# Graph kernel on one core: gathers that land in the tile of use, an ordering moved into the gate stage, and a node table that carries its degree factor

## The chip, the core and the metric
The kernel runs on one core of one Trainium2 chip. The metric is the device time of one execution in microseconds. The engines are TensorE (PE, with its weight loads as PEld), VectorE (DVE), ScalarE (ACT), GpSimd (POOL) and SyncE (SP); L-numbers are lines of the kernel's file.

## What is computed
100,000 nodes with 48 features, 25,000 edges (src, dst), the edges ordered by dst. Four layers, each added to its input and normalised over the 48 features:

```python
x = LN(x + L0(x)); x = LN(x + L1(x)); x = LN(x + L2(x)); x = LN(x + L3(x))
# L0: (1+eps)*x + segment_sum(relu(x[src] + ea48), dst)
# L1: msg = x[src] * rsqrt(max(out_deg,1))[src]
#     agg = segment_sum(msg, dst) * rsqrt(max(in_deg,1))
#     relu(where(in_deg>0, agg, x) @ W.T + b)
# L2: dis = rsqrt(deg) where deg>0 else 0 (deg counts src)
#     relu(segment_sum(dis[src]*dis[dst]*x[dst], src) @ W.T + b)
# L3: gate = silu(ea40 @ W1.T + b1) @ W2.T + b2
#     gate += sum(emb[type[src]] * (emb[type[dst]] @ adaptW.T))
#     msg = gate * h[dst] * (cutoff(weight) * node_vec[dst])
#     h + segment_sum(msg, src) / max(segment_sum(node_vec[dst], src), 1e-8), layer norm, gamma, beta
```

## The kernel before, in words
**Layout.** The edges lie as 128 partitions x 196 columns (`EP = 25088`), handled in 14 chunks of H = 14 columns or 7 blocks of R = 28. The nodes are 28 dense blocks of 128 x 28 x 48, worked in pairs (h = 0, 1). Node tables in DRAM: `xa_table` (XA: x, type, place and degree of each node, 52 wide), `x_table` and `y_table` (X1, Y1: the state after layer 0 and the same times the degree factor, 48 wide; X2 after layer 1), `edge_records`, `records_by_src`, `h_by_src` for layers 2 and 3.

**Gathers and scatters.** A gather of 128 rows is one indirect DMA, issued by GpSimd; a whole one is 196 of them. All gathers go through `ring`, two halves of 14 columns: `gather_turn` (L420) waits for `ring_free`, issues 14 DMAs into half c % 2, and a consumer empties it. For the gathers of x by src, of XA by dst and of X2 by src the consumer is ScalarE: `source_rows` (L606), the loop with `take` (L555) and `rows_of_src` copy the half to `XS`, `zs`, `nv`, `zd`, `place` and `dg`, and give the half back. For the gather of y it is `take_terms` (L535), which writes the transposed terms that VectorE's scan reads. A scatter (`scatter`, L456) sends 14 rows of `stage`, which ScalarE fills in `to_stage` (L594) from M or XS, and only rows that are the last of their segment are written.

**The stages in order of time.** (a) VectorE counts sources by 196 comparisons of one column with 128 numbers (`L1179`), a product of one-hots on TensorE gives the degree of each node; meanwhile GpSimd gathers x by src. (b) ScalarE writes the degrees into the node rows that SP streams through `din` (`degrees`, L616), SP stores XA; meanwhile VectorE orders the edges by source: `sort` (L1042), a bitonic network of 120 comparisons (two instructions each, L1065 and L1066) and 14 turns by TensorE on the array `va`/`vb`, which lies inside the tile `do`. (c) VectorE sums the messages of layer 0 (L1218 and a scan, 14 times). (d) Pass 1: norm of x for all nodes, times `deg` for Y1 (L1303), two stores per block; beside it GpSimd gathers XA by dst. (e) Seven update blocks (`xs` of the nodes at dst; the product by the root of the degree) and the scatter of y; pass 2, which multiplies each block of X1 by the weights on TensorE and stores X2, runs beside the scatter. (f) The gather of y and the gate of layer 3: 49 groups of four columns. In a group VectorE makes the two one-hots of the next group (L1359), TensorE transposes them (L933), multiplies by `logit` (L945), by the first weights (L950) and by the second (L955), and VectorE combines (L1372 to L1379). In groups 0 and 4 of each block VectorE also scans the terms of one chunk. (g) Updates, the scatter into X2; (h) gather of the records, ordering of them; gather of X2 by src, of H2 into `ring`, the last sums and the scatter into the output.

**What sets the order.** Every engine runs its own program, written out in this order; they meet in semaphores only. SP issues the loads and stores of `din` and `do`/`dy` in a fixed sequence, also the store of the ordered keys (`SRT`) before pass 1.

```python
            def gather_turn(table, w, of, c, **skip):
...
            def take(h, uses):

                act.wait_ge(fill[h].sem, fill[h].up(H))
                for to, of in uses:
                    nc.scalar.activation(to, of, ACT.Copy).then_inc(own.sem, own.add())
                act.wait_ge(own.sem, own.now())
                act.sem_inc(S["ring_free"], 1)
                act.sem_inc(S["kept"], 1)
```

## Time and profile before

| | |
|---|---|
| runs | 3299.1, 3349.46 and 3291.38 us (median 3299.1) |
| profiled execution | 3287.26 us, span 3285.5 us |
| busy, share of the span | POOL 59%, DVE 62%, PE 23%, ACT 19% |
| the chain that ended last | DVE 28%, POOL 24%, issue 19%, PE 12%, another core or an unknown queue 9%, ACT 5%, DMA 3% |
| DMA | mean 82 GB/s; 56,448 packets of indirect DMAs |

POOL's busy time is the time of its 1768 instructions, the greater part of them issues of indirect DMAs. "Issue" in the chain is time in which the engine waited for nothing that the profile shows. "Another core or an unknown queue" stands for a release whose origin the profile can't name; on a group of rows it reads "remote". The clock of TensorE is granted at 0.5 of full speed in most slices.

### The profile page before, as it was taken

Reading aid. Unit: us, or ns where it says so; the run is one execution under the profiler, and the core shown is the slowest. Engines: PE = TensorE matmul, PEld = TensorE weight load, DVE = VectorE, ACT = ScalarE, POOL = GpSimd, SP = SyncE. Lnnn points to the kernel's source line nnn. Section 1 sums busy time; section 2 is a strip of 40 time slices with the busy share of each in tenths; the row PEclk is TensorE's granted clock in tenths of the full one; section 3 lists DMA queues with packets and bytes.
Section 4 is the critical chain, followed back from the end, with each engine's and each line's share of the span. In section 5 each row is a group of like instructions: output and inputs, shape, how many; then the busy total and the mean of one; then the engine's idle time right before and its main releaser. Section 6 shows DMA issues by size and latency. Waiting matters only on the chain.

```text
span 3285.5 us, 13920 instructions
## 1 busy us (share of the span) xinstructions
PE 766.0 (23%) x3478; PEld 542.8 (17%) x3478; DVE 2024.3 (62%) x2590; ACT 622.5 (19%) x1021; POOL 1932.9 (59%) x1768
## 2 busy tenths in 40 slices
PE   1182000000166663877742300000340000000000
PEld 0020000000155552544431300000340000000000
DVE  2186279977865564545452470788658969948551
ACT  0000101221122231322211100222111223221110
POOL 5704623774055657564326773777757777673776
PEclk7586555555565565555555555555555555555555
DMA  3106703763033331110000099344222212210000
GB/s 110 21 1 243 277 27 137 273 223 144 0 108 109 131 120 56 26 25 22 20 10 14 15 82 85 117 135 135 76 69 67 83 57 80 66 52 7 16 15 15
DMA packets 154357, 268.53 MB, mean 82 GB/s; under 512 B 87656, under 2 KB 112314, under 8 KB 154146
## 3 DMA queue, kind: packets, MB, share of 16 engines
q1 hardware_dynamic: 92786, 198.90, 20.8%
q0 software_dynamic: 56448, 44.04, 6.7%
q10 hardware_dynamic: 5040, 24.69, 2.0%
q8 instruction: 28, 0.46, 0.1%
q14 instruction: 55, 0.45, 0.0%
HBM read 135.62 MB, written 137.21 MB: 83 GB/s over the span
## 4 chain that ended last, share of the span: by engine, by line
DVE 28%; POOL 24%; issue 19%; PE 12%; another core or an unknown queue 9%; ACT 5%; DMA 3%; SPq 0%; ACTq 0%; DVEq 0%; POOLq 0%
POOL ring L424 10%; POOL out L462 6%; POOL x_table L462 5%; POOL y_table L462 3%; DVE mu L1259 2%; DVE var L1268 2%; DVE du L1262 2%; PE psA L897 2%; DVE sumb L1205 2%; PE psO L859 2%; PE psA L950 1%; PE psT L844 1%; DVE du L1471 1%; DVE do L1467 1%
## 5 line engine op out<-in xcount | busy, mean ns | idle before, releaser
L462 POOL DMA_INDIRECT y_table<-sumb,put x196 | 214.7, 1095 | 258.6 <-ACT sumb L594 201.0
L462 POOL DMA_INDIRECT x_table<-sumb,put x196 | 216.4, 1104 | 180.6 <-ACT sumb L594 117.8
L424 POOL DMA_INDIRECT ring<-xa_table,dstI x196 | 216.9, 1106 | 171.9 <-ACTq L561 101.7
L424 POOL DMA_INDIRECT ring<-in_xaux,srcI x196 | 186.3, 950 | 207.9 <-ACTq L561 116.8
L424 POOL DMA_INDIRECT ring<-edge_records,dstI x196 | 227.9, 1163 | 102.0 <-issue 61.3
L424 POOL DMA_INDIRECT ring<-y_table,srcI x196 | 201.4, 1028 | 137.6 <-ACTq L544 78.9
L424 POOL DMA_INDIRECT ring<-h_by_src,zd x196 | 230.1, 1174 | 87.4 <-issue 61.0
L424 POOL DMA_INDIRECT ring<-x_table,srcI x196 | 224.4, 1145 | 90.9 <-issue 58.1
L462 POOL DMA_INDIRECT out<-sumb,put x196 | 214.6, 1095 | 106.8 <-issue 60.8
L1268 DVE TENSOR_REDUCE var<-sq 128x28 f32<-128x1344 f32 x119 | 181.1, 1551 | 143.0 <-ACT sq L567 142.8
L830 PE MATMUL psG<-ident,tail 128*49 128x128 f32 x10 | 4.3, 433 | 1086.9 <-DVEq L1011 1086.9
L567 ACT ACTIVATE sq<-du 128x1344 f32<-128x1344 f32 x126 | 164.5, 1320 | 450.5 <-DVE du L1262 420.2
L830 PEld LDWEIGHTS psG<-ident,tail 128*49 128x49 f32 x10 | 1.5, 154 | 1089.3 <-DVEq L1011 1072.9
L844 PE MATMUL psT<-ident,din 128*96 128x128 f32 x392 | 96.1, 395 | 294.8 <-DMA din<-x_table 294.6
L586 ACT ACTIVATE hT<-psT 96x512 f32<-96x512 f32 (+1 forms) x168 | 88.8, 537 | 377.2 <-PE psT L844 190.3
L859 PE MATMUL psO<-w1b,hT 97*128 97x96 f32 x504 | 107.6, 386 | 147.1 <-ACT hT L586 141.0
L1179 DVE TENSOR_SCALAR GX<-GX 128x128 bf16<-128x128 int16 x196 | 49.3, 252 | 125.1 <-remote 113.3
L859 PEld LDWEIGHTS psO<-w1b,hT 97*128 97x128 f32 x504 | 99.8, 295 | 155.9 <-ACT hT L586 147.4
L844 PEld LDWEIGHTS psT<-ident,din 128*96 128x96 f32 x392 | 73.0, 200 | 298.0 <-DMA din<-x_table 295.8
L1259 DVE TENSOR_REDUCE mu<-du 128x28 f32<-128x1344 f32 x70 | 106.1, 1549 | 3.0
L1262 DVE SCALAR_TENSOR_TENSOR du<-mu,du 128x1344 f32<-128x1344 f32 x70 | 106.6, 1555 | 1.4
L1205 DVE TENSOR_TENSOR_SCAN sumb<-mask,sub 128x720 f32<-128x720 bf16 x56 | 92.8, 1657 | 17.3 <-ACT sub L528 9.1
(280 smaller groups left out, 3013.9 us busy)
## 6 DMA issues: line engine op xcount, KB each, us to landing
din<-in_xaux SPq DMA_DIRECT2D x56, 728.0 KB
x_table<-do SPq DMA_DIRECT2D x56, 672.0 KB
din<-x_table SPq DMA_DIRECT2D x56, 672.0 KB
xa_table<-din SPq DMA_DIRECT2D x28, 728.0 KB
y_table<-GX SPq DMA_DIRECT2D x28, 672.0 KB
out<-do SPq DMA_DIRECT2D x28, 672.0 KB
records_by_src<-ring ACTq DMA_DIRECT2D x14, 693.0 KB
GX<-records_by_src ACTq DMA_DIRECT2D x14, 693.0 KB
```

The lines of the kernel that those rows point to most:

```text
L424: pool.indirect_dma_start(ring[:, h, t, 0:w], None, table, bass.IndirectOffsetOnAxis(ap=of[:, c * H + t:c * H + t + 1], axis=0), **skip).t ...
L462: pool.indirect_dma_start(table, bass.IndirectOffsetOnAxis(ap=put[:, c * H + t:c * H + t + 1], axis=0), stage[:, h, t, :], None, bounds_ch ...
L567: nc.scalar.activation(sq[:, h, :, :], u, ACT.Square).then_inc(S["squared"], 1)
L586: nc.scalar.activation(hT[0:96, g % 2, 0:w], psT[g % 2][0:96, 0:w], ACT.Copy).then_inc(S["hT_ready"], 1)
L844: last = T.transpose(psT[g % 2][0:96, j * P:(j + 1) * P], rows_of[:, (4 * g + j) * 96:(4 * g + j + 1) * 96], ident[:, :])
L859: last = T.matmul(psO[k % 6][:, j * 96:(j + 1) * 96], hT[0:97, g % 2, j * P:(j + 1) * P], weights[:, :], start=True, stop=True)
L897: last = T.matmul((psA, psB)[c][:, 0:CN // 2], ohp[:, g, :], ohc[:, g, c * (CN // 2):(c + 1) * (CN // 2)], start=start, stop=stop, skip_gr ...
L1179: V.tensor_scalar(ohp[:, g, :], iota[:, 0:P], parf[:, bass.ds(i * R + t, 1)], None, ALU.is_equal)
L1205: return V.tensor_tensor_scan(sums_row[:, part], mask_row, terms_row[:, part], 0.0, ALU.mult, ALU.add)
L1259: V.tensor_reduce(mu[:, h, :], x, X, ALU.add).then_inc(own.sem, own.add())
L1262: V.scalar_tensor_tensor(u, along(mu[:, h, :]), -1.0 / D, x, ALU.mult, ALU.add).then_inc(S["centered"], 1)
L1268: V.tensor_reduce(var[:, h, :], sq[:, h, :, :], X, ALU.add).then_inc(S["var_ready"], 1)
```

## The change
It does three things. The three node gathers named above land at once in one tile, `XD` (128 x 196 x 52), of which `XS` is the first 48 columns: `gather_in_place` has one semaphore for each chunk (`rows0` to `rows13`) and no ring half. The gather of XA waits at each chunk for `xs_free` (the sum of layer 0 over this chunk is done), that of X2 for `by_src` (the ordering of the records). The copies of ScalarE for them are gone. The ordering by source leaves stage (b) and becomes a generator, of which VectorE does up to six steps ahead of each of the gate's 49 groups; the turns by TensorE come at 14 fixed groups; the keys are stored behind the gate. `deg` is turned into the degree factor before XA is built, X1 and `x1_with_degree` (Y1) are 49 wide and hold x and the factor; the two products (L1303, and `M` by the root) are gone, VectorE multiplies the messages by the factor as it forms the terms in the gate (`messages`), and pass 2 multiplies by `w1c`, which has a zero row for the factor. ScalarE stages the rows of the y scatter between the updates (`STAGED`) and between the pairs of pass 2 (`STAGED_LATER`).

```diff
+            rows, xs_free = views(*ROWS), views("xs_free")[0]
+            def gather_in_place(table, w, of, free=None):
+                for c in range(CE // H):
+                    if free:
+                        pool.wait_ge(free.sem, free.up())
+                    for t in range(c * H, c * H + H):
+                        pool.indirect_dma_start(
+                            XD[:, t, 0:w], None, table, bass.IndirectOffsetOnAxis(ap=of[:, t:t + 1], axis=0)
+                                ).then_inc(rows[c].sem, rows[c].add())
...
-            gather(A["xaux"], XW, srcI)
+            gather_in_place(A["xaux"], XW, srcI)
             pool.wait_ge(S["xa_done"], 1)
-            gather(XA, XW, dstI)
+            gather_in_place(XA, XW, dstI, xs_free)
             pool.wait_ge(idx_ready.sem, idx_ready.up())
             pool.wait_ge(short_done.sem, short_done.up())
-            scatter(Y1)
-            gather(Y1, D, srcI)
+            scatter(Y1, stage1)
+            gather(Y1, YW, srcI)
...
+            def to_stage1(i):
+                act.wait_ge(rows_new.sem, rows_new.up())
+                for h in range(2):
+                    cols = bass.ds((2 * i + h) * H, H)
+                    act.wait_ge(stage_free.sem, stage_free.up())
+                    nc.scalar.activation(stage1[:, h, :, 0:D], XS[:, cols, :], ACT.Copy).then_inc(own.sem, own.add())
+                    nc.scalar.activation(stage1[:, h, :, D], XD[:, cols, D + 3], ACT.Copy).then_inc(own.sem, own.add())
+                    act.wait_ge(own.sem, own.now())
+                    act.sem_inc(S["rows_ready"], 1)
+            STAGED = {0: 0, 3: 1, 6: 2}
             for i in range(NBLK):
                 norm([(0, su[:, :, :])])
+                if i in STAGED:
+                    to_stage1(STAGED[i])
+            STAGED_LATER = {1: 3, 2: 4, 4: 5, 5: 6}
...
+            one(V.tensor_scalar(none, deg, 1.0, None, ALU.min))
+            one(V.tensor_scalar(deg, deg, 1.0, None, ALU.max))
+            ask_act()
+            one(V.reciprocal(deg, deg))
+            one(V.tensor_tensor(deg, deg, none, ALU.mult))
             dve.sem_inc(S["deg_done"], 1)
...
-            sort(own, ask_pe)
-            dve.sem_inc(S["srt_ready"], 1)
...
                     for h in range(2):
-                        V.tensor_tensor(dy[:, h, :, :], DO[h],
-                                        along(deg[:, bass.ds((PER * i + 2 * q + h) * R, R)]), ALU.mult
-                                        ).then_inc(S["out_ready"], 1)
+                        V.tensor_copy(do1[:, h, :, D], deg[:, bass.ds((PER * i + 2 * q + h) * R, R)]
+                                      ).then_inc(own.sem, own.add())
...
+            ordering, turns = sort(own, ask, answered, pos2), sort_groups()
+            def sort_on(g):
+                if g + 1 in turns:
+                    return
+                for _ in range(QUOTA):
+                    if next(ordering, "end") in ("turn", "end"):
+                        break
+            def factors(g):
+                sort_on(g)
+                if g + 1 < GROUPS:
+                    one_hots(g + 1)
+                if g % (R // 4) in (0, 4):
+                    messages(g % (R // 4) // 4)
...
+            def messages(h):
+                dve.wait_ge(fill[h].sem, fill[h].up(H))
+                V.tensor_tensor(terms[:, h, :, 1:H + 1].rearrange("p d c -> p c d"), ring[:, h, :, 0:D],
+                                along(ring[:, h, :, D]), ALU.mult).then_inc(ring_read.sem, ring_read.add())
+                dve.wait_ge(ring_read.sem, ring_read.now())
+                dve.sem_inc(S["ring_free"], 1)
+                summed(h, 2)
```

GpSimd at its first gather and the start of the second, before (`srcI` and `dstI` are the indices, `xa_done` SP's word that XA is stored):

```order
19 L424 DMA ring<-in_xaux,srcI 128x52 [waits ring_free,edges]
20 L424 DMA ring<-in_xaux,srcI 128x52 x13
21 L424 DMA ring<-in_xaux,srcI 128x52 [waits ring_free]
22 L424 DMA ring<-in_xaux,srcI 128x52 x13
23 L424 DMA ring<-in_xaux,srcI 128x52 [waits ring_free]
...
47 L424 DMA ring<-xa_table,dstI 128x52 [waits xa_done,ring_free,fill1,fill0]
48 L424 DMA ring<-xa_table,dstI 128x52 x13
49 L424 DMA ring<-xa_table,dstI 128x52 [waits ring_free]
```

GpSimd at the same place after the change:

```order
19 L465 DMA XD<-in_xaux,srcI 128x52 [waits edges]
20 L465 DMA XD<-in_xaux,srcI 128x52 x195
21 L465 DMA XD<-xa_table,dstI 128x52 [waits xs_free,xa_done]
22 L465 DMA XD<-xa_table,dstI 128x52 x13
23 L465 DMA XD<-xa_table,dstI 128x52 [waits xs_free]
```

The first gather has no wait between its 196 DMAs any more, the second waits for the sums of layer 0 in place of the ring.

VectorE behind the degrees, before (`GX` holds the degrees and ranks there, `do` the array being ordered):

```order
776 L1193 TENSOR_SCALAR GX<-deg 128x784 [waits dve]
777 L1194 TENSOR_SCALAR GX<-GX,carry 128x784 [waits dve]
778 L1195 TENSOR_TENSOR GX<-GX 128x784 [waits dve]
779 L1048 CAST do<-do 98x256 [waits dve]
780 L1049 MEMSET do 32x256 [waits dve]
781 L1050 TENSOR_SCALAR do<-do 98x256 [waits dve]
```

VectorE at the same place after the change:

```order
779 L1215 TENSOR_TENSOR GX<-GX 128x784 [waits dve]
780 L1216 TENSOR_SCALAR GX<-GX 128x784 [waits dve]
781 L1217 TENSOR_SCALAR GX<-GX 128x784 [waits dve]
782 L1219 RECIPROCAL GX<-GX 128x784 [waits dve,act_done]
783 L1220 TENSOR_TENSOR GX<-GX 128x784 [waits dve]
784 L1240 TENSOR_TENSOR sub<-MG,XD 128x14x48 [waits dve,rows0,ea48]
785 L1243 CAST mask<-cont 128x48x14
```

The factor stands ahead of the release of ScalarE's copy, and the sums of layer 0 follow at once, without the ordering.

VectorE in the gate, one group before (`L1359` makes the one-hots of the next group):

```order
1612 L1359 TENSOR_TENSOR du<-iotaz,du 128x480 [waits dve]
1613 L1359 TENSOR_TENSOR sq<-iotaz,du 128x480
1614 L1372 TENSOR_TENSOR sq<-psB,sq 128x480 [waits dve,mlp_o]
1615 L1374 TENSOR_REDUCE lg<-sq 128x4 [waits dve]
1616 L1376 TENSOR_TENSOR do<-psG,lg 128x192 [waits mlp_g,dve]
1617 L1379 TENSOR_TENSOR GX<-do,t1 128x4x48 [waits dve]
```

VectorE in the gate, one group with steps of the ordering after the change (one-hots are `L1380`):

```order
1370 L1082 TENSOR_SCALAR do<-do 128x16x8 [waits dve]
1371 L1082 TENSOR_SCALAR do<-do 128x8x16 [waits dve]
1372 L1070 TENSOR_TENSOR do<-do 128x16x8 [waits dve]
1373 L1071 TENSOR_TENSOR do<-do 128x16x8
1374 L1070 TENSOR_TENSOR do<-do 128x32x4 [waits dve]
1375 L1071 TENSOR_TENSOR do<-do 128x32x4
1376 L1380 TENSOR_TENSOR du<-iotaz,du 128x480 [waits dve]
1377 L1380 TENSOR_TENSOR sq<-iotaz,du 128x480
1378 L1410 TENSOR_TENSOR sq<-psC,sq 128x480 [waits dve,mlp_o]
1379 L1412 TENSOR_REDUCE lg<-sq 128x4 [waits dve]
1380 L1414 TENSOR_TENSOR do<-psT1,lg 128x192 [waits mlp_g,dve]
1381 L1417 TENSOR_TENSOR GX<-do,t1 128x4x48 [waits dve]
```

The steps stand ahead of the one-hots, for which TensorE waits; a group can hold six of them.

## Rows read from the trace of the kernel before

**Rows 1.** Groups by line: busy us, mean ns of one, idle us before them with releasers.

```profile
L424 POOL DMA_INDIRECT ring<-xa_table,dstI x196 | 216.9, 1106 | 171.9 <-ACTq L561 101.7 <-issue 64.6 <-SPq L336 5.6
L462 POOL DMA_INDIRECT y_table<-sumb,put x196 | 214.7, 1095 | 258.6 <-ACT sumb L594 201.0 <-issue 57.6
L424 POOL DMA_INDIRECT ring<-in_xaux,srcI x196 | 186.3, 950 | 207.9 <-ACTq L561 116.8 <-issue 67.4 <-DMA do<-in_src 23.7
...
L1179 DVE TENSOR_SCALAR GX<-GX 128x128 bf16<-128x128 int16 x196 | 49.3, 252 | 125.1 <-remote 113.3 <-issue 8.5 <-PE psB L897 3.0
```

**Rows 2.** Stretches: length, then busy us of PE, PEld, DVE, ACT, POOL, clock, DMA.

```profile
526.00:785.00 259.00, 0.00 (x0) 0.00 (x0) 219.78 (x168) 63.26 (x121) 190.19 (x168) 0.50 0.67 237
900.00:1257.00 357.00, 220.83 (x1140) 203.67 (x1139) 224.54 (x246) 106.08 (x176) 214.71 (x196) 0.61 0.33 113
1271.00:1640.00 369.00, 263.14 (x1195) 166.07 (x1195) 169.63 (x287) 105.45 (x149) 191.58 (x188) 0.50 0.11 24
```

**Rows 3.** Stretches of L1179 alone (counts): length, DVE busy (x), clock, DMA.

```profile
41.00:179.00 138.00, 7.05 (x26) 0.51 0.11 19
179.00:261.00 82.00, 39.84 (x160) 0.95 0.00 1
```

**Rows 4.** Timeline of VectorE, two comparisons: start us, us, instruction, idle before.

```profile
330.61 0.29 DVE L1065 TENSOR_TENSOR do<-do 128x128 f32<-128x128 f32 x1 [1.61 <-remote]
...
404.60 0.29 DVE L1065 TENSOR_TENSOR do<-do 128x128 f32<-128x128 f32 x1
```

**Rows 5.** Stretches of L1259 alone (one for each norm of a block).

```profile
797.00:886.80 89.80, 9.32 (x6) 0.50 0.00 0
1016.90:1052.10 35.20, 3.01 (x2) 0.50 0.27 91
1052.10:1069.00 16.90, 3.01 (x2) 0.85 0.32 115
```

**Rows 6.** Timeline from the degrees to pass 1, ScalarE, GpSimd and VectorE.

```profile
268.77 0.26 ACT L616 ACTIVATE din<-GX 128x28 f32<-128x28 f32 x1 [137.03 <-DVEq L1196]
...
400.21 0.94 POOL L424 DMA_INDIRECT ring<-xa_table,dstI  x1 [5.59 <-SPq L336]
...
516.86 5.05 DVE L1233 RECIPROCAL deg<-deg 128x784 f32<-128x784 f32 x1 [0.98 <-ACT deg L600]
```

**Rows 7.** Stretch of L616 alone (degrees into node rows, two a pair of blocks).

```profile
277.00:303.00 26.00, 1.56 (x6) 0.50 0.95 350
```

**Rows 8.** Stretches of L1303 alone (two a pair), and last one of L1218.

```profile
538.90:651.40 112.50, 21.18 (x14) 0.50 0.78 278
651.40:793.00 141.60, 21.19 (x14) 0.50 0.61 219
...
446.00:516.00 70.00, 18.18 (x14) 0.50 0.06 23
```

**Rows 9.** Timeline of TensorE and VectorE in one group of the gate.

```profile
1609.56 1.94 PE L955 MATMUL psT<-wm,do 49*128 49x48 f32 x8 [0.26 <-ACT do L679]
1611.43 1.38 PE L945 MATMUL psO<-logit,do 120*128 120x120 bf16 x12
1612.74 1.94 PE L950 MATMUL psA<-din,wm 40*48 40x512 f32 x2
1613.09 0.65 DVE L1359 TENSOR_TENSOR sq<-iotaz,du 128x480 bf16<-128x480 bf16 x1
1614.61 0.68 PE L933 MATMUL psO<-identb,du 128*120 128x128 bf16 x4
```

**Rows 10.** Groups by line: the terms of y by ScalarE, the sum in layer 0.

```profile
L540 ACT ACTIVATE sub<-ring 128x672 f32<-128x672 f32 x14 | 20.0, 1431 | 7.0 <-DMA ring<-y_table,srcI 6.5
L1218 DVE TENSOR_TENSOR sub<-MG,XS 128x672 f32<-128x672 f32 x14 | 18.2, 1298 | 0.7 <-DVE do L1066 0.2
```

**Rows 11.** Timeline of VectorE at the update of layer 2 and the last sums.

```profile
2470.44 1.56 DVE L1524 TENSOR_TENSOR du<-XS,MG 128x1344 f32<-128x1344 f32 x1 [10.75 <-ACTq L756]
...
2662.92 0.86 DVE L1535 TENSOR_TENSOR du<-ring,GX 128x672 f32<-128x672 f32 x1 [11.37 <-DMA ring<-h_by_src,zd]
```

More of the change, by code:

```diff
@@ L20 @@
 XW = 52
+YW = D + 1
 RW = 99
@@ L223, in bass_gnn @@
         psO = [ps("psO0"), ps("psO1"), psA, psB, psC, psG]
+        ROWS = tuple(f"rows{c}" for c in range(CE // H))
         S = {n: sem(n) for n in (
@@ L447, in gather_records, with scatter @@
                     gather_turn(REC, RW, of, c)
-            def gather_x2(of):
-                for c in range(2):
-                    ring_used(c)
-                    gather_turn(X2, D, of, c)
-                gather(X2, D, of, first=2)
-            def scatter(table):
+            def scatter(table, rows_of=stage):
                 for c in range(CE // H):
@@ L1385, in _ @@
+            for g in range(GROUPS):
+                factors(g)
+            for _ in ordering:
+                pass
+            dve.sem_inc(S["srt_ready"], 1)
             dve.wait_ge(returned.sem, returned.up(2 * NBLK))
```

439 lines of the change are left out of this document (213 added, 226 removed).

## The prediction
> **What bounds the kernel now.** I read the page's groups first. GpSimd issues nine rounds of 196 indirect DMAs, seldom more than 0.3 us apart, and stands still only where another engine holds it up: 116.8 us in the first gather (a free ring half, which ScalarE gives), 101.7 us in the second (the same), 201.0 us in the y scatter (staged rows) [rows 1]. The undisturbed pace is (186.3+67.4)/196 = 1.29 us, and between instructions 1.25 us. Nine rounds at 1.25 to 1.45 us are 2205 to 2558 of 3285 us, so no single engine is the bound: the chain hands over from stage to stage. Next the stages [rows 2]: pass 1 (526 to 785) has VectorE at 220 of 259 us; pass 2 (900 to 1257) and the gate (1271 to 1640) have no full engine. There the rows in time matter. A count takes 0.51 us when GpSimd is silent (160 in 82 us) and 5.3 us while it gathers (26 in 138 us) [rows 3], and of the 125.1 us that the counts' line stood idle 113.3 are put down to "remote" [rows 1]. A comparison of the ordering (two instructions) takes 0.53 us when undisturbed and 2.1 us next to table copy and gather, 1.61 of it again "remote" [rows 4]. A pair of pass 2 took 35.2 us under a scatter and 16.9 us with GpSimd idle [rows 5]. I read this as one effect: **while GpSimd issues without a pause, streams of short instructions on the other engines are starved**, some 17 us after it starts and up to 15 us after it stops (counting was slow from 41 to 179 us, GpSimd issued from 24 to 164 us). Long instructions aren't touched: pass 1 kept its pitch under 164 us of gathering. The change removes the pauses of GpSimd, so this effect decides.
>
> **Step 1, the count and the first gather.** The gather no longer waits for ring halves; it runs from 24.2 us for 196 x 1.25 = 245 us, to 269 instead of 164 us with a second part later. That removes the wait of 116.8 us, but not from the path: who ends last is the count, since the table copy needs degrees. In 105 us more of gathering 105/5 = 21 counts are made, which take 10.5 us otherwise: +94 us. The trace has no count under a longer gather; the bounds are 0 (only the first 140 us starve) and +105 (nothing is done); the row is the same gather, so +94. The degree factor (two TENSOR_SCALARs, a root, the reciprocal of 784 columns, a product) now stands ahead of the copy: the reciprocal alone is 5.1 us [rows 6], with the rest +8. Degrees are ready at 268.7+94+8 = 371 us.
>
> The Trainium skill ("Runtime: NRT & Kernel Launch", section "Instruction fetch mechanics") says that instructions are streamed in blocks by a DMA queue of the engine's own and that this fetch is mostly hidden. By that rule alone short streams would not slow, and the count would end as before; that is rival A below.
>
> **Step 2, the table copy.** 268.8 to 400.2 us before, 131 us or 9.4 a pair of blocks [rows 6]. Its first three pairs, mostly without the gather, took 26 us, 8.7 each, with DMA at 0.95 [rows 7]. Now nothing is gathered beside it: 14 x 8.5 = 118 us (bounds 118 and 131). The copy ends at 489 us, +89. The ordering by source is gone from VectorE here, and the sums of layer 0 (14 of them, 70 us [rows 8]) fit under the copy: nothing.
>
> **Step 3, pass 1 and the second gather.** Pass 1 begins at 494 us (before 525.8). A pair of blocks took 16.1 us (seven in 112.5), then 20.2 us (seven in 141.6) where ScalarE stood in take() for rows [rows 8]; both go, and so does the product for y: 2 x 1.51 = 3.0 us less (21.18 us for 14), 0.4 us for two short copies: 13.5 us x 14 = 189 us, end 683 (at 14.5 us: 697). DMA has room: 0.67 share at 259 us [rows 2] is 173 us of work. The gather runs beside it at 1.45 us: 285 us, 489 to 774 us. Before it ended at 785: **a wait of 101.7 us is gone, yet only 11 us are won**, for the start is later. What is won is behind it: the seven update blocks (15.0 us each, six in 89.8 [rows 5], 13.5 without the product for y) lie under the gather, so the scatter starts at 776, not 900.7 us: -125 us for GpSimd.
>
> **Step 4, staging.** ScalarE stages block 1 in the middle of the updates and needs the ring halves that the scatter frees. The first is free when chunk 0 has landed (776+22), the second after chunk 1 (817). Until then ScalarE squares nothing, VectorE waits in update 4 (it would be there at 740). Updates 4 to 6 end at 850, the second half of block 2 at 857; pass 2 starts then, against 893 us: -36 us. The lead of 125 us shrinks, since the scatter at 1.40 us a DMA rules the stage.
>
> **Step 5, pass 2.** GpSimd now scatters without the 83 us in which it waited, and gathers two chunks of y behind: busy from 857 to some 1120 us, short waits for staging included. At 31 us a pair (between 22.5 and 35.2) that is 8.4 pairs, the other 5.6 at 17 us: end at 1215, with ScalarE's waits for halves 1225 us, as against 1262 us: **-37**, no more. Bounds: 1185 (25 us) to 1250 us. In the product the 97th row of a transpose costs nothing visible.
>
> **Step 6, the gate.** Undisturbed, a group is 6.0 us, all TensorE: 1.94+1.38+1.94+0.68 [rows 9]. 49 groups are 294 us; the stage took 369, so 75 us are starvation, 28 of them in one burst of 42 gathers. Now each of 34 groups gets up to six steps of the ordering between GX of the last group and the one-hots of the next. TensorE waits for these one-hots; their slack is 0.9 us (ready at 1613.7, used at 1614.61). The 165 steps are 120 comparisons x 0.53, 14 copies and some 31 short ones: 79 us; 34 x 0.9 = 30 us are hidden, so +50 us. Transposes for the turns: 14 x 0.9, half hidden, +5. The messages move from ScalarE (1.43 us) to VectorE (1.30 us, the row of the like sum of layer 0) [rows 10]: a group can hide 2.4 us of it, a group with steps 1.3: +20 us. Of starvation the long burst goes (-28), but VectorE issues nearly twice as many instructions while GpSimd gathers (18 of 29 us a chunk): I take 70 us, bounds 0 and 150. Sum: 294+50+5+20+70 = 439 us, **+70**. The stage ends at 1232+439 = 1671, before at 1640: +31.
>
> **Step 7, the rest.** One root, one reciprocal of 196 columns and three short operations are gone ahead of the third scatter: -4 us. Storing the ordered keys moves behind the gate on SP's queue, beside updates that wait for nothing of SP: 0 (bound +4). The last gather of x2 goes in place: VectorE's wait of 10.75 us goes and the h2 gather starts some 33 us earlier, which saves the two waits of 11.4 us [rows 11]; its own pace then holds the second chunk: -28 us at the dense pairs, and so at the end. Against it, the product stage there (84 TensorE rows in 15 us) loses the pauses of GpSimd: +8 (0 to 30).
>
> **The sum**: -39 up to the gate (-37 and 2 us of its head), +70, -4, -20 = **+7 us** on 3287 us of the profiled execution, which lies 12 us under the median of 3299. I predict 3294 us, no difference that can be told. (Some 2%, 66 us, is what a measurement of this kernel separates from no change.)
>
> **Rivals.** A: the count isn't slowed by a longer gather. For it: it recovered at 179 us by itself, and 440 instructions then ran at full speed, the last 20 us of them beside a gather. Against: each stretch of slow counts lies within GpSimd's issuing plus 15 us. Then all to the third scatter comes 94 us earlier: 3200 us. It decides once the extra delay stays under 20 us. Chance 0.2.
> B, slower: the ordering is starved in the gate as it was beside the table copy. 120 comparisons at 2.1 instead of 0.53 us are +188 us; the gate has GpSimd silent for a third of the time, so +125, less the 30 us I have already put in for it: 3390 us. For it: the ordering's instructions are as short as the counts, and they stand in the stage with the most of them. Against: pauses of 5 us were enough to refill. It decides when a comparison costs over 1.0 us on average. Chance 0.17.
> C: pass 2 and gate go on at undisturbed speed, for starvation belongs to the table traffic: pass 2 ends at 857+14 x 18 = 1110, gate 369 us: 3294-115-70 = 3110 us. The slow pair at 35.2 us with DMA at a third speaks against it: 0.04.
>
> **Chances.** 0.59 for mine (3230 to 3360 by the bounds of steps 5 and 6). The range takes in A and most of B: 3200 to 3385. Faster by over 2%: A, C and a tail of mine, 0.26; within 2%: 0.53; slower: 0.21.
>
> **What would show it.** First gather ends near 269 us with no wait; degrees at 370 us (A: 277); copy's end at 489; first y scatter at 776; update 4 of pass 1 waiting some 70 us for ScalarE; first matmul of pass 2 at 857; gate from 1232 to 1671, groups with steps 8.2 us apart; h2 gather 33 us nearer to the record gather's end. I am wrong if the counts keep 0.5 us after 180 us, or if the gate is far from 439 us.

## The result and the profile after
The changed kernel took 3524.2 us (median of 4 runs, 3508.4 to 3545.4), the kernel before 3324.3 us (median of 4, 3291.4 to 3377.1): ratio 1.070, 95% interval 1.060 to 1.080. It is slower by 7%; I had forecast no difference, 3294 us. The profiled execution took 3508.4 us (span 3506.6), 221 us more than the 3287.3 us of the one before. In two of the experiments below, e5 and f4, one of the four executions was slow by over 4%; the medians given contain it (3150.7 and 3064.1 us without it), the ratios don't.

The groups by line of the profile after, GpSimd's first and then two of VectorE's (busy us, mean ns, idle us before them with releasers); they answer to [rows 1]:

```profile
L452 POOL DMA_INDIRECT ring<-h_by_src,zs x196 | 233.4, 1191 | 317.9 <-ACTq L783 186.4 <-DMA h_by_src<-MG 73.6 <-issue 57.9
...
L465 POOL DMA_INDIRECT XD<-xa_table,dstI x196 | 221.5, 1130 | 292.6 <-SPq L361 233.2 <-issue 59.4
...
L495 POOL DMA_INDIRECT x_with_degree<-sumb,put x196 | 200.3, 1022 | 106.1 <-issue 60.5 <-ACTq L647 45.5
L465 POOL DMA_INDIRECT XD<-x_table,srcI x196 | 191.4, 977 | 59.8 <-issue 59.8
L465 POOL DMA_INDIRECT XD<-in_xaux,srcI x196 | 188.1, 960 | 85.2 <-issue 60.0 <-DMA t<-in_ew 25.1
...
L1199 DVE TENSOR_SCALAR GX<-GX 128x128 bf16<-128x128 int16 x196 | 51.5, 263 | 228.3 <-remote 177.6 <-issue 48.0 <-PE psB L892 2.5
L1557 DVE TENSOR_SCALAR MG<-psO 128x384 f32<-128x384 f32 x14 | 7.8, 558 | 178.7 <-remote 111.5 <-issue 39.6 <-PE psO L854 27.6
```

The three in-place gathers wait for no ring half any more, as the change says: apart from the first start (25.1 us) and the wait for the table copy, their idle time is "issue". What was 116.8 and 101.7 us of waiting for ring halves is gone. In its place stand 233.2 us for the table copy, and in the last gather (H2) 73.6 us for the stored products and 186.4 us for ring halves, where before 24.1 and 2.3 us were waited. The counts (L1199) stood idle 228.3 us, before 125.1. The last row is the product stage of layer 2, in which TensorE multiplies seven blocks while X2 is gathered: its 14 rows waited 178.7 us. In the kernel before the same group reads:

```profile
L1515 DVE TENSOR_SCALAR MG<-psO 128x384 f32<-128x384 f32 x14 | 7.8, 557 | 43.9 <-PE psO L859 40.2 <-remote 3.7
```

The stretches of the two lines in the profile after: counts in the first two rows ([rows 3] of before), the product stage in the third:

```profile
41.00:290.00 249.00, 14.05 (x50) 0.51 0.12 21
300.00:369.00 69.00, 35.46 (x138) 0.97 0.00 1
...
2394.00:2692.00 298.00, 13.21 (x26) 0.50 0.12 29
```

50 counts in 249 us, 5.0 us each, and 138 in 69 us, 0.50 each, once GpSimd (silent from 273.7 us) lets go. The product stage took 298 us for what it did in 94 us before (2343 to 2437 us). The points that the prediction named, in time, with their idle times:

```profile
385.35 0.26 ACT L626 ACTIVATE din<-GX 128x28 f32<-128x28 f32 x1 [6.19 <-DVEq L1221]
...
506.88 0.95 POOL L465 DMA_INDIRECT XD<-xa_table,dstI  x1 [233.16 <-SPq L361]
...
788.14 1.01 POOL L495 DMA_INDIRECT x_with_degree<-sumb,put  x1 [0.31 <-issue]
...
827.34 1.55 DVE L1287 TENSOR_REDUCE var<-sq 128x28 f32<-128x1344 f32 x1 [60.33 <-ACT sq L582]
...
866.94 2.02 PE L854 MATMUL psO<-w1c,hT 98*128 98x96 f32 x8 [146.62 <-ACT hT L601]
...
1317.96 0.65 PE L922 MATMUL psO<-identb,du 128*120 128x128 bf16 x4 [24.53 <-DVEq L1383]
...
2698.35 1.89 POOL L452 DMA_INDIRECT ring<-h_by_src,zs  x1 [73.58 <-DMA h_by_src<-MG]
...
2898.17 1.47 POOL L452 DMA_INDIRECT ring<-h_by_src,zs  x1 [154.30 <-ACTq L783]
```

Read down: degrees at 385 us (forecast 371), copy done by 507 (489), scatter of y at 788 (776), the wait of 60 us in an update for ScalarE (forecast some 70), pass 2 at 867 (857): up to here the forecast holds within 18 us. The gate began at 1317 us (forecast 1232). It ended at 1722 us, and in the kernel before at 1651 us: 71 us behind. When the gather of X2 begins the kernel is 51 us behind the one before (2373.9 against 2323.0 us); my sum had +27 there. The rest, 170 us, arises behind it, where my sum had -20. Its terms are in the rows: 73.6 + 186.4 - 24.1 - 2.3 = 234 us more waiting of the H2 gather, less 64 us by which the gather of X2 is shorter (251 against 315 us), 170 us. The norms and dense pairs (2698 to 2898 us), which had lain beside the gather of X2, now lay behind the late product stage, and the ring halves could only be refilled after them.

How the product stage crawls, in the timeline of ScalarE, VectorE and TensorE (start, us, instruction, idle before). TensorE transposes `sub` in lots of four (`psT`), ScalarE copies them to `hT`, TensorE multiplies `hT` into `psO`, `psA` or `psB`, and VectorE takes the product out:

```profile
2447.32 0.36 DVE L1557 TENSOR_SCALAR MG<-psB 128x192 f32<-128x192 f32 x1 [10.64 <-issue]
...
2452.67 1.94 PE L840 MATMUL psT<-ident,sub 128*96 128x128 f32 x8 [31.78 <-issue]
2458.51 0.59 ACT L601 ACTIVATE hT<-psT 96x512 f32<-96x512 f32 x1 [38.85 <-issue]
2459.16 2.02 PE L854 MATMUL psO<-w2b,hT 97*128 97x96 f32 x8 [4.54 <-issue]
2460.98 1.06 PE L840 MATMUL psT<-ident,sub 128*96 128x128 f32 x4
2469.72 0.59 ACT L601 ACTIVATE hT<-psT 96x512 f32<-96x512 f32 x1 [10.61 <-issue]
...
2492.11 0.56 DVE L1557 TENSOR_SCALAR MG<-psO 128x384 f32<-128x384 f32 x1 [39.55 <-issue]
2503.32 0.59 ACT L601 ACTIVATE hT<-psT 96x512 f32<-96x512 f32 x1 [33.01 <-issue]
...
2525.72 0.56 DVE L1557 TENSOR_SCALAR MG<-psO 128x384 f32<-128x384 f32 x1 [33.04 <-remote]
2531.32 0.38 ACT L601 ACTIVATE hT<-psT 96x256 f32<-96x256 f32 x1 [27.41 <-remote]
...
2553.72 0.56 DVE L1557 TENSOR_SCALAR MG<-psA 128x384 f32<-128x384 f32 x1 [27.44 <-remote]
2564.91 0.36 DVE L1557 TENSOR_SCALAR MG<-psB 128x192 f32<-128x192 f32 x1 [10.64 <-remote]
```

TensorE starts 0.06 us after ScalarE's copy has ended (2459.10), so that direction isn't slow. The other one is. The eight transposes of 2452.67 us are two lots of four; ScalarE copies the first 4.8 us after its end by the profile (2453.8) and the second 15.1 us after (2454.6 to 2469.7), though it stood idle for 10.6 us of that. VectorE takes the first product 30.9 us after it ended by the profile (2461.2 to 2492.1).

The starts follow a simple count. ScalarE and VectorE go on at intervals of 11.2, 22.4, 11.2, 22.4, 5.6, 22.4 and 11.2 us (2458.51 to 2564.91), and between the results that they wait for lie 4, 8, 4, 8, 2, 8 and 4 instructions of TensorE (transposes or products): **2.8 us for each instruction of TensorE**, for transposes and products alike. A count is two of its instructions, and takes 5.6 us (VectorE starts them at 104.32, 109.91, 115.52 us). A block of this stage is 42, and the last result of one block and of the next are taken at 2447.32 and 2564.91 us: 117.6 us, 42 times 2.8. The traces of a and f1 below have the same intervals. The semaphore events in the trace say on which side the delay lies: while counts crawl, TensorE's signal is given 4.1 us after its product has ended by the profile (median of 42 counts; 0.01 us where nothing crawls), and VectorE starts 0.02 us after the signal. So the waiting engine is ready and the signal is late. The profile models the ends of TensorE's instructions, so whether the result or only its signal is late can't be told from it.

### The profile page after: what moved, and what is told of

It is laid out like the page before. It is cut to its first block, busy times and chain, and to the rows that moved or that the text cites. A ratio compares the mean times of both kernels' runs of the same rounds, so it can differ in the third digit from the quotient of the medians.

```text
span 3506.6 us, 13765 instructions
## 1 busy us (share of the span) xinstructions
PE 780.9 (22%) x3478; PEld 560.1 (16%) x3478; DVE 1996.2 (57%) x2610; ACT 569.2 (16%) x906; POOL 1899.0 (54%) x1768
## 3 DMA queue, kind: packets, MB, share of 16 engines
q1 hardware_dynamic: 93060, 200.27, 19.3%
## 4 chain that ended last, share of the span: by engine, by line
DVE 25%; POOL 23%; issue 20%; another core or an unknown queue 13%; PE 10%; DMA 5%; ACT 4%; SPq 0%; ACTq 0%; DVEq 0%; POOLq 0%
POOL XD L465 6%; POOL out L495 6%; POOL x_table L495 5%; POOL ring L452 3%; POOL x_with_degree L495 3%; DVE mu L1278 2%; DVE du L1281 2%; DVE var L1287 2%; DMA din<-in_xaux 2%; PE psT L840 2%; PE psO L854 2%; DMA xa_table<-din 1%; PE psA L892 1%; DVE do L1512 1%
## 5 line engine op out<-in xcount | busy, mean ns | idle before, releaser
L452 POOL DMA_INDIRECT ring<-x_with_degree,srcI x196 | 205.5, 1048 | 376.4 <-DVEq L1426 318.5
L452 POOL DMA_INDIRECT ring<-h_by_src,zs x196 | 233.4, 1191 | 317.9 <-ACTq L783 186.4
L465 POOL DMA_INDIRECT XD<-xa_table,dstI x196 | 221.5, 1130 | 292.6 <-SPq L361 233.2
L495 POOL DMA_INDIRECT x_with_degree<-sumb,put x196 | 200.3, 1022 | 106.1 <-issue 60.5
L465 POOL DMA_INDIRECT XD<-in_xaux,srcI x196 | 188.1, 960 | 85.2 <-issue 60.0
L465 POOL DMA_INDIRECT XD<-x_table,srcI x196 | 191.4, 977 | 59.8 <-issue 59.8
L601 ACT ACTIVATE hT<-psT 97x512 f32<-97x512 f32 (+3 forms) x168 | 88.9, 540 | 598.7 <-remote 220.0
L1199 DVE TENSOR_SCALAR GX<-GX 128x128 bf16<-128x128 int16 x196 | 51.5, 263 | 228.3 <-remote 177.6
L840 PE MATMUL psT<-ident,din 128*97 128x128 f32 x392 | 98.6, 401 | 273.6 <-DMA din<-x_table 273.4
L854 PE MATMUL psO<-w1c,hT 98*128 98x96 f32 x392 | 85.0, 392 | 250.6 <-ACT hT L601 201.1
L840 PEld LDWEIGHTS psT<-ident,din 128*97 128x97 f32 x392 | 79.6, 267 | 275.6 <-DMA din<-x_table 275.6
L1557 DVE TENSOR_SCALAR MG<-psO 128x384 f32<-128x384 f32 x14 | 7.8, 558 | 178.7 <-remote 111.5
```

The costliest lines, as they stand in the source:

```text
L452: pool.indirect_dma_start(ring[:, h, t, 0:w], None, table, bass.IndirectOffsetOnAxis(ap=of[:, c * H + t:c * H + t + 1], axis=0), **skip).t ...
L465: pool.indirect_dma_start(XD[:, t, 0:w], None, table, bass.IndirectOffsetOnAxis(ap=of[:, t:t + 1], axis=0)).then_inc(rows[c].sem, rows[c]. ...
L495: pool.indirect_dma_start(table, bass.IndirectOffsetOnAxis(ap=put[:, c * H + t:c * H + t + 1], axis=0), rows_of[:, h, t, :], None, bounds_ ...
L601: nc.scalar.activation(hT[0:tall, g % 2, 0:w], psT[g % 2][0:tall, 0:w], ACT.Copy).then_inc(S["hT_ready"], 1)
L840: last = T.transpose(psT[g % 2][0:tall, j * P:(j + 1) * P], rows_of[:, at:at + tall], ident[:, :])
L854: last = T.matmul(psO[k % 6][:, j * 96:(j + 1) * 96], hT[0:tall + 1, g % 2, j * P:(j + 1) * P], weights[:, :], start=True, stop=True)
```

## The experiments
**Two kinds of chip.** The executions fell on several chips, and they differ. On some the kernel before takes 3177 to 3324 us (medians) and shows the 5 us counts; on others it takes 2905 to 2919 us and counts take 0.5 us under the gather. I call the first kind starving, and set the ratio only between runs taken together on one chip. The five groups of experiments ran on five chips, one after the other, and none of these came twice: that the difference belongs to the chip, and not to the hour, is my reading and not shown. The first four experiments fell on a chip that doesn't starve, so what they expected of starvation could not be seen there; they gave something else, the price of each part without it.

**Hold in the gather of X2 (e1), hold in the first gather (e2), both (e4).** The edit, on the changed kernel:

```diff
                 for c in range(CE // H):
+                    if c in holds:
+                        pool.wait_ge(S[holds[c][0]], holds[c][1])
...
+            gather_in_place(A["xaux"], XW, srcI, holds={8: ("deg_done", 1)})          # e2, e4
+            gather_in_place(X2, D, srcI, holds={2: ("h2_ready", 2), 3: ("h2_ready", 4), 4: ("h2_ready", 6),
+                                                5: ("h2_ready", 7)})                  # e1, e4
```

> The changed kernel, but in the in-place gather of X2 chunks 2, 3, 4 and 5 wait until blocks 2, 4, 6 and 7 of the product stage are done, as the ring made them wait before. Theory S (unbroken issuing by GpSimd starves short instructions): the product stage takes 106 to 125 us in place of 315 us, the gather of X2 315 us in place of 251 us, so the gather of H2 starts at about 2700 us as now but is no longer held for 154 us; its end comes 160 to 180 us earlier, the kernel takes 3330 to 3350 us. Theory R (the loss sits in the prefilled ring halves and the order of ScalarE's work, not in the stream): the product stage shortens by less than 60 us or the hold of 154 us stays, and the time stays above 3450 us.

> The changed kernel, but the first gather stops after eight chunks (112 DMAs) until the degrees are ready. Theory S: counts recover at about 180 us, the degrees and their factor are ready at 277 us in place of 385, the table copy takes 131 us in place of 118, the scatter of y starts at 690 to 700 us in place of 788; the kernel takes 3405 to 3430 us. The rival (the lead is lost again in pass 2 and the gate, where other things end last): scatter of y at 700, but the kernel stays over 3480 us.

> The changed kernel with both holds, in the first gather and in the gather of X2. If both losses are starvation and add up, 3230 to 3265 us, some 1% under the kernel before (3287 us profiled). If the rest of the change is a loss of its own, over 3300 us.

Measured, not starving: e1 2946.4 us, ratio 1.012 (1.010 to 1.014); e2 2923.2 us, 1.0045 (1.003 to 1.006); e4 2947.3 us, 1.013 (1.011 to 1.015). The hold of e2 is void there: the degrees are ready at 155 us, before the gather comes to chunk 8 (its 196 DMAs run from 25.3 to 293.9 us with no gap), so e2 stands for the changed kernel. Where nothing starves, then, the change costs 12 us, and holding the gather of X2 costs 23 us more and gives nothing. What the three runs were to decide, how much each hold gives back, stayed undecided there.

**The ordering behind the gate (e3).**

```diff
-                if g + 1 in turns:
+                if g < GROUPS:
                     return
```

(and TensorE's 14 turns behind its last group).

> The changed kernel with all 165 steps of the ordering and its 14 turns in one piece behind the last group of the gate, where GpSimd is silent. My working of the prediction: the gate's groups shorten by 55 us (from 405 to 350 us), and the ordering costs 105 to 115 us by itself: 50 to 60 us slower in all, 3560 to 3585 us. Rival (the steps are starved inside the gate): the gate's groups shorten by more than 100 us, and the time is the same as the changed kernel or less.

Measured: 2951.5 us, ratio 1.014 (1.011 to 1.017). The gate of e2 and of e3 in stretches (length, then PE, PEld, DVE, ACT, POOL busy, clock, DMA), first e2, with its pass 2:

```profile
650.00:969.00 319.00, 222.41 (x1166) 214.78 (x1167) 214.51 (x239) 103.78 (x179) 170.83 (x166) 0.61 0.37 124
993.00:1342.00 349.00, 279.37 (x1268) 178.68 (x1268) 270.27 (x599) 89.48 (x138) 178.46 (x168) 0.50 0.13 24
```

and e3:

```profile
990.00:1278.00 288.00, 273.12 (x1240) 172.53 (x1240) 195.17 (x314) 84.90 (x137) 183.59 (x168) 0.50 0.16 29
```

The steps cost the groups 61 us (I had 50 + 5), and 14 us of 75 us of VectorE's work (270.27 - 195.17) are hidden in them. Behind the gate the ordering makes the kernel 28 us slower than inside (expected 50 to 60). That bears out my working of the steps' own cost. It says nothing on the rival, starved steps, for nothing starves on this chip; f3, f4, e6 and e9 below decide that.

**The kernels on a starving chip (b, a, e4b, e5).** The edit of e5, waits for landing in the in-place gathers:

```diff
                                 ).then_inc(rows[c].sem, rows[c].add())
+                    pool.wait_ge(rows[c].sem, rows[c].now())
```

> The kernel before, unchanged, for a trace beside the experiments. Two conditions are possible. Where short instructions are starved while GpSimd issues (as in the two traces that I compared): 3290 to 3350 us, counts at 5 us under the gather. Where they are not (as in the first four experiments, where the kernel before took 2912 us): 2905 to 2915 us, counts at 0.5 us throughout.

> The changed kernel, unchanged. Starved: 3500 to 3545 us, ratio 1.06 to 1.08. Not starved: the product stage takes some 91 us under the gather of X2, the gate's groups 350 us, and the time is that of the run with a hold in the first gather, 2915 to 2930 us, ratio 1.00 to 1.01, since without starvation this hold ends before the gather comes to it.

> Both holds again. Starved: 3230 to 3265 us if both losses are starvation and add up, over 3300 us if the rest of the change is a loss of its own. Not starved: 2940 to 2950 us, 25 us over the changed kernel, which is the price of the hold in the gather of X2.

> The changed kernel, but GpSimd waits after each chunk of 14 in-place DMAs until they have landed, some 2 us, 42 pauses in three gathers. Starved, theory S with short pauses enough to refill: counts and products recover by half or more, 3300 to 3400 us. Starved, theory S with only long pauses enough: within 30 us of the changed kernel plus 80 us. Not starved: 42 pauses of 2 us lie on GpSimd's own path, 60 to 90 us slower than the changed kernel.

Measured: the kernel before 3177.4 us (its own run with a trace 3188.1); the changed kernel 3479.4 us, ratio 1.095 (1.089 to 1.100); both holds 3185.4 us, 1.002 (0.998 to 1.007); waits for landing 3170.3 us, 0.996 (0.988 to 1.003). Both holds take 294 us from the changed kernel; the recorded 3230 to 3265 us were 243 to 278 us under the 3508 us of the first profile. The counts and the product stage by line, the changed kernel on this chip:

```profile
L1199 DVE TENSOR_SCALAR GX<-GX 128x128 bf16<-128x128 int16 x196 | 50.9, 260 | 228.0 <-remote 179.8 <-issue 44.3 <-PE psB L892 3.8
...
L1557 DVE TENSOR_SCALAR MG<-psO 128x384 f32<-128x384 f32 x14 | 7.8, 558 | 179.2 <-remote 112.1 <-issue 41.5 <-PE psO L854 25.6
```

and e5, with 14 pauses in each gather:

```profile
L1200 DVE TENSOR_SCALAR GX<-GX 128x128 bf16<-128x128 int16 x196 | 49.9, 255 | 57.8 <-PE psB L893 54.2 <-remote 1.1 <-issue 0.8
...
L1558 DVE TENSOR_SCALAR MG<-psO 128x384 f32<-128x384 f32 x14 | 7.8, 558 | 41.3 <-PE psO L855 29.6 <-issue 11.7
```

The "remote" waits of the counts fell from 179.8 to 1.1 us, those of the products from 112.1 us to none. In stretches, the changed kernel's counts under the gather and its product stage:

```profile
41.00:290.00 249.00, 14.12 (x51) 0.51 0.14 21
...
2365.00:2662.00 297.00, 13.09 (x26) 0.50 0.14 29
```

the same of e5:

```profile
41.00:202.00 161.00, 47.77 (x188) 0.69 0.14 21
...
2260.00:2352.00 92.00, 13.30 (x26) 0.50 0.23 62
```

and the product stage of e3, on the chip that doesn't starve and with no pause at all in the gather of X2:

```profile
2046.00:2138.00 92.00, 13.30 (x26) 0.50 0.24 64
```

The landing waits stop GpSimd for 1.6 to 2.6 us after each 14 DMAs in these stretches; the whole first gather took 300.7 against 247.9 us, some 4 us a chunk. They give the product stage its full speed back, though the gather of X2 still puts 196 DMAs into 304 us (252 without them). The counts come back to 0.86 us each (188 in 161 us), not to the 0.51 of e3. In e4b the gather keeps its pace within each burst and stops 4 to 9 us after 28, 14 and 14 DMAs, and its product stage takes 95 us, as that of e5. So the length of GpSimd's run without a stop decides here, more than the amount gathered, and the theory with short pauses enough holds, further than I expected (3300 to 3400 us).

**Pauses in the scatter and gather of y (e6, f3), the ordering early (e7), both (e9, f4), pauses in the kernel before (e8, g1).** The edits:

```diff
+                    if land:                                    # scatter(Y1): after each chunk
+                        pool.wait_ge(sc[h].sem, sc[h].now())
...
+                    if land:                                    # gather(Y1): after each chunk
+                        pool.wait_ge(fill[c % 2].sem, fill[c % 2].now())
...
+            for _ in sort(own, ask, answered, pos):             # e7, e9: ahead of the sums of layer 0
+                pass
+            dve.sem_inc(S["srt_ready"], 1)
```

> The changed kernel with GpSimd waiting for the landing of each chunk of 14, now also in the scatter and the gather of y. Starved condition: pass 2 (744 to 1158 us in the run with waits in the in-place gathers alone, 323 us long where nothing is starved) falls from 414 to 340 us, the gate from 404 to 350 to 365 us; the scatter is 24 us longer on GpSimd; some 80 to 110 us less than the run with waits in the in-place gathers alone, ratio to the kernel before 0.965 to 0.98. Rival (the rest of these stages is not starvation but the order of staging and of the ordering's steps): within 20 us of that run, ratio 0.99 to 1.00. Not starved: 20 to 40 us slower than the changed kernel.

> The changed kernel with landing waits in the in-place gathers and the ordering by source back ahead of the sums of layer 0, its store back ahead of pass 1. The gate loses the steps: from 404 us (starved) to about 320 us as before, or from 349 to 290 us where nothing is starved. Pass 1 starts some 45 us later, since 90 us of ordering and 70 us of sums stand against 128 us of table copy. Starved: 40 us less than with the steps in the gate, ratio 0.98 to 0.99. Rival (the steps in the gate are hidden behind TensorE): 30 to 45 us more, ratio 1.00 to 1.01.

> The kernel before with the same waits for landing in its gathers of x, XA, y and X2 and in its scatter of y. Starved: counts end at about 200 us in place of 260, but the first gather still stands behind ScalarE; pass 2 and the gate lose 20 to 40 us each: ratio 0.96 to 0.98. Rival (the ring's own pauses did this already): 0.99 to 1.01. Not starved: 30 us slower.

> The changed kernel with landing waits in the in-place gathers and in the scatter and the gather of y, and the ordering ahead of the sums of layer 0. If both gains add up, some 130 us less than the run with waits in the in-place gathers alone: ratio 0.95 to 0.965 where starved; if they are one and the same (steps in the gate only cost because they starve), no better than the better of the two alone.

These four fell on a chip that doesn't starve: e6 3028.8 us, ratio 1.040 (1.038 to 1.042); e7 2963.2, 1.018 (1.016 to 1.021); e8 2978.3, 1.023 (1.021 to 1.025); e9 2967.8, 1.019 (1.017 to 1.021). There pauses only cost, more than I gave them: 106 us against e2 in place of 20 to 40 (on two chips; the kernel before ran 2911.6 and 2910.5 us on them), and 68 us on the kernel before (e8) in place of 30. The ordering ahead of the sums takes 61 us off e6, and the gate goes from 349 us (e6) to 289 (e9). The questions of starvation stayed open, so four more runs followed:

> The changed kernel, unchanged. Starved: ratio 1.06 to 1.10. Not starved: 2915 to 2930 us, ratio 1.00 to 1.01 as with the hold in the first gather, which there ends before the gather comes to it.

> The kernel before, for its trace beside the others. Not starved: 2910 us, the gate about 300 us (49 groups of 6.0 us), pass 2 about 250 us (14 pairs of 17 to 18 us), so that the changed kernel's gate of 349 us is 50 us longer, the steps of the ordering alone. Starved: 3180 to 3300 us, the gate 323 to 370 us.

> The changed kernel with landing waits also in the scatter and the gather of y. Starved: the gate and pass 2 come down to within 15 us of their lengths where nothing is starved (349 and 323 us) if all of their excess is starvation by this traffic; ratio 0.96 to 0.99. If the order of staging and steps makes them long, ratio over 1.0. Not starved: ratio 1.04 as measured.

> The same with the ordering ahead of the sums of layer 0. Starved: 30 to 60 us less than with the steps in the gate, ratio 0.94 to 0.97. Not starved: ratio 1.02 as measured.

This was a starving chip. The kernel before 3236.8 us, the changed kernel 3487.1 us, ratio 1.078 (1.070 to 1.085); with all pauses (f3) 3116.0 us, 0.963 (0.957 to 0.969); with the ordering early besides (f4) 3069.2 us, 0.9485 (0.941 to 0.956). Pass 2 and the gate in stretches, the kernel before (f2):

```profile
811.00:1162.00 351.00, 233.06 (x1168) 212.30 (x1168) 218.38 (x243) 106.22 (x177) 217.64 (x200) 0.59 0.35 115
1185.00:1550.00 365.00, 272.88 (x1240) 172.38 (x1240) 177.58 (x301) 106.14 (x151) 179.45 (x175) 0.50 0.13 24
```

the changed kernel (f1):

```profile
869.00:1261.00 392.00, 237.12 (x1168) 222.74 (x1168) 215.57 (x241) 104.90 (x180) 169.75 (x167) 0.57 0.31 101
1284.00:1682.00 398.00, 280.13 (x1268) 178.45 (x1268) 270.84 (x600) 89.91 (x138) 179.14 (x168) 0.50 0.12 21
```

with all pauses (f3):

```profile
733.00:1063.00 330.00, 237.48 (x1168) 226.22 (x1168) 215.99 (x242) 103.94 (x180) 170.90 (x165) 0.57 0.37 121
1086.00:1484.00 398.00, 280.30 (x1270) 178.71 (x1271) 270.79 (x600) 89.90 (x138) 173.26 (x168) 0.50 0.12 21
```

and with the ordering early (f4):

```profile
742.00:1070.00 328.00, 231.56 (x1168) 221.03 (x1168) 215.39 (x241) 103.28 (x179) 172.55 (x165) 0.58 0.37 122
1093.00:1428.00 335.00, 273.41 (x1240) 172.52 (x1240) 195.41 (x315) 86.34 (x137) 178.50 (x168) 0.50 0.14 25
```

Pass 2 fell from 392 to 330 us, which is within 11 us of e2's 319 where nothing starves: its excess was starvation, by the scatter and the first chunks of y. The gate did not move, 398 us with the pauses and without, against 349 us where nothing starves. There my expectation fell. The y gather had gone in bursts of 14 or 28 with 6 to 19 us between them in the gate already (f1), and waits begin inside a burst; one row of f3, a wait from 1203.9 to 1212.8 us with a burst from 1191.9 to 1210.2 us:

```profile
1212.81 0.36 DVE L1419 TENSOR_TENSOR do<-psT,lg 128x192 f32<-128x192 f32 x1 [8.88 <-remote]
```

What the gate gives back is the ordering: 63 us (398 to 335). Pass 2 starts 9 us later for it, and 47 us are left in all. On the chip that doesn't starve the same move took 60 us from the gate (349 to 289), so starvation of the steps themselves is worth 3 us. The comparisons of the ordering in the gate show it directly, in the first profile of the changed kernel (240 instructions, half of them on this line and half on the next):

```profile
L1070 DVE TENSOR_TENSOR do<-do 128x128 f32<-128x128 f32 x120 | 35.1, 293 | 4.2
```

They never waited more than 0.04 us.

The last two runs:

> The kernel before with landing waits in its gathers of x, XA, y and X2 and in the scatter of y. Starved: if the pauses alone make the gain, ratio 0.95 to 0.97 and the change itself is worth nothing there; if the change needs them and they need the change, 0.98 to 1.0. Not starved: 1.02 as measured.

> The kernel before, for its trace beside the last. Not starved: the gate about 300 us, pass 2 about 250 us. Starved: as in the earlier traces, 323 to 370 us for the gate.

They fell on a chip that doesn't starve: g1 2973.7 us, ratio 1.020 (1.018 to 1.022), and g2 2915.3 us. So whether the kernel before would gain as much from pauses alone on a starving chip wasn't measured. The trace of g2 gives its stages, pass 2 and gate:

```profile
692.00:975.00 283.00, 214.81 (x1153) 204.73 (x1154) 216.99 (x242) 104.97 (x177) 205.95 (x186) 0.64 0.42 139
998.00:1296.00 298.00, 272.50 (x1240) 172.37 (x1240) 178.24 (x302) 105.01 (x151) 200.02 (x191) 0.50 0.16 30
```

Both kernels, where nothing starves and where it does (us from the span's start; the changed kernel without starvation is e2; the profiled execution of f2 was 40 us below the median of the kernel before on its chip, so the last two columns differ by more than the medians):

| | before, g2 | changed, e2 | before, f2 | changed, f1 |
|---|---|---|---|---|
| last count | 135 | 138 | 259 | 369 |
| table copy ends | 276 | 288 | 402 | 507 |
| gather of XA ends | 582 | 571 | 701 | 790 |
| pass 2 starts | 692 | 650 | 811 | 869 |
| gate | 998 to 1296 | 993 to 1342 | 1185 to 1550 | 1284 to 1682 |
| gather of X2 ends | 2266 | 2275 | 2547 | 2613 |
| product stage | 1975 to 2065 | 2018 to 2106 | 2252 to 2345 | 2382 to 2679 |
| scatter into the output starts | 2630 | 2638 | 2911 | 3210 |

Without starvation the change does what it is built for up to pass 2 (42 us earlier), loses 36 us in pass 2 (319 against 283), where ScalarE now waits for scatter halves between pairs (12.3, 19.3 and 17.3 us ahead of its copies L646; three pairs took 32 to 39 us, all others 17 to 23), 51 us in the gate, and wins 34 us in the gather of X2: +8 us at the end.

## Why the prediction was wrong
**Step 7 failed, by 190 of the 214 us.** I had forecast +7 us and got +221 us. I costed the product stage at "+8 (0 to 30)" and took the earlier H2 gather for a gain of 28 us. The stage took 298 us in place of 94 us, +204, and the H2 gather was held by it. The other 24 us arose before the gather of X2 began. I had the effect in hand: step 1 charged 94 us to the same cause, an unbroken gather beside work that passes through TensorE. In the kernel before, the gather of X2 stopped for 5.6, 10.5, 10.5 and 3.4 us after 28, 14, 14 and 14 DMAs, just while the product stage ran, and the stage was nearly undisturbed; I scaled its small rest of waiting instead of asking what the first gather showed for an unbroken stream. The counts gave 5.3 us for two instructions of TensorE; at 2.8 us each the 42 of a block are 118 us, and the 251 us of the gather hold two blocks. The pauses of e5 and e4b, which break the stream, remove the whole loss (3479 to 3170 and 3185 us).

**The mechanism was named too widely.** The prediction says that streams of short instructions on the other engines are starved. What is late is what TensorE hands on; short instructions of VectorE alone kept their pace in the gate (the row above), and chains between VectorE and ScalarE kept it in pass 1. The slow comparisons of [rows 4] are another matter: beside the table copy and a gather in bursts of 14 and 28, the comparisons of the kernel before waited 71 us in all, 16 us in b and 4 us (nothing unusual) in f2.

**Steps 1 to 4 were right.** Gather's end 273.7 us (269), degrees 385 (371), copy 507 (489), pass 1 at 13.8 us a pair (13.5), scatter 788 (776), update 4 waiting 60 us (70), pass 2 at 867 (857). The count cost 108 us (94). The counts under a longer gather stayed at 5.0 us, and rival A is out where it starves; e5's 188 counts in 161 us under a gather with pauses bear that out.

**Step 5 was too small.** Pass 2 and its end: 426 us from 867 to 1293, I had 368. Two things are in it: six pairs under the scatter and the first y chunks instead of 8.4, which is starvation (the pauses take 62 us from pass 2 in f3), and pairs of some 19 us behind it, not 17, of which the profile shows no single cause. One of the six pairs took 106 us, beside 84 DMAs (1020.9 to 1131.0 us) with a single stop of 2 us; there too VectorE's waits for TensorE are 32 to 33 us long.

**Step 6 had the total roughly, by terms that were off.** The gate took 405 us (forecast 439). Without starvation the steps cost 61 us (forecast 55). The messages on VectorE cost nothing: e3's gate without steps takes 288 us, that of the kernel before 298 (g2, on another chip that doesn't starve), where I had +20. Starvation is 56 us over e2's 349, where I had 70. The stage of the kernel before is misread in the prediction as well: at 1640 us nearly two groups were still to come, as its matmuls show (x1195, against 1240 in g2), and the gate took 380 us:

```profile
1271.00:1651.00 380.00, 273.88 (x1244) 172.81 (x1244) 177.54 (x300) 106.89 (x152) 191.58 (x188) 0.50 0.11 23
```

So the gate became 25 us longer, not 70. Rival B named the gate as the place where starvation would grow by 125 us, once a comparison costs over 1.0 us. It wasn't and they didn't: starvation is 49 to 56 us in the changed gate (398 to 405 against 349 us) and 25 to 82 us in the one before (323 in b, 365 in f2 and 380 us, against 298), in the three sets of traces that starve. That B's time, 3390 us, lies nearer to the measured one than mine is luck: the loss came from another stage.

**The rule of the Trainium skill** ("Runtime: NRT & Kernel Launch", section "Instruction fetch mechanics") says that the fetch of instructions is mostly hidden; by it short streams would have run on. On the chips that starve, short streams behind TensorE don't run on; on those that don't, where 189 counts took 97 us under an unbroken gather, nothing speaks against it. VectorE started 0.02 us after each late signal, so it had its instruction at hand: a late fetch on its side is not what the counts waited for, and the rule itself is neither borne out nor refuted.

**Open:** what in the chip holds back TensorE's results or signals while GpSimd issues; why some chips do it and others don't, or whether one chip always does; what delayed the comparisons of [rows 4]; and what the pauses would give to the kernel before where it starves. Every execution on record has its span and clock from the profiler, so no run shows whether the effect is there without it.

## What to carry to other kernels
A wait of GpSimd that looks like waste can be what lets the other engines run: before removing the pauses in a long row of indirect DMAs, look what runs beside it, and if it passes from TensorE to another engine every few microseconds, try a wait for landing after each 14 or so. Count the instructions of TensorE in that stage: here each cost 2.8 us for as long as the stream went on. When one stage of a trace shows such an effect, charge it to every stage in which the change makes the same condition, also those where the old pauses hid it. And run both kernels on more than one chip: the same change cost 0.4% on one and 7 to 9% on others, and the version with pauses and the early ordering was 5% faster than the kernel before on one and 2% slower on another.

## What the runs showed of the hardware
- One kernel took up to 14% longer on some chips than on others: the kernel before took 2911 to 2916 us on three (counts 0.5 us under a gather) and 3177 to 3324 us on the starving ones (counts 5 us). There GpSimd's own pace was no worse: its first unbroken gather took 247 to 248 us for 196 DMAs, against 265 to 269 us on the other kind.
- While GpSimd issued without a stop on a starving chip, results passed out of TensorE at 2.8 us for each of its instructions: 5.6 us for the two of a count, 117.6 us for the 42 of a block. Its signals came up to 58 us after the end that the profile gives (2472.8 to 2531.3). ScalarE's signals to TensorE were not late (0.06 us).
- Pass 1, which passes only between VectorE and ScalarE, ran at 13.8 us a pair under 281 us of unbroken gathering on the starving chip, and at 13.9 us on the other.
- A stop of 1.6 to 2.6 us after each 14 DMAs gave the product stage its full speed (92 us) and the counts most of it: 188 in 161 us in place of 51 in 249 us. In the gate, with bursts of 14 and pauses between them, 49 us of starvation stayed.
- TensorE's granted clock followed: 0.51 of full speed (the 1.2 GHz level) while it stood waiting in the starved count, 1.00 in the same stretch where nothing starves, read off e3:

```profile
41.00:138.00 97.00, 45.57 (x189) 1.00 0.16 26
```
